# Two more tiles of a gate/up stage by seven block products, and a down dequantization moved into the turns of the tiles

## The chip, the cores and the metric

The kernel runs on one core of a Trainium2 chip. The metric is the device time of one execution in microseconds. Engines: TensorE (PE), VectorE (DVE), ScalarE (ACT), GpSimd (POOL), and SyncE (SP), which only issues DMA.

## What is computed

Two layers, each a residual addition of a conditioned projection and a gated feed-forward. The change touches the first layer's feed-forward. Cut to what matters:

```
GROUP = 128; HIDDEN = 512; INTER = 1376
def _dequant(qw, qz, sc, g_idx):      # 8 nibbles in a word
    wq = unpack_rows(qw); zq = unpack_cols(qz) + 1.0
    return sc[g_idx] * (wq - zq[g_idx])

y = base(x) + 2 * lora(x)                      # 1024 tokens, 512 wide
w_gu = _dequant(qweight_gu, qzeros_gu, scales_gu, g_idx_gu)
gate, up = split(y @ w_gu, INTER)
h = silu(gate) * up
w_d = _dequant(qweight_down, qzeros_down, scales_down, g_idx_down)
x = x + h @ w_d
x = x + layer1(x)     # per-batch 512x512 projection, RMS norm, gated feed-forward of 1792
```

## The kernel before

Everything is computed transposed: features lie on the 128 partitions, the 1024 tokens in two halves of 512 columns. INTER is padded to 11 tiles of 128 (`FT0 = 11`). A float32 product is made of three matmuls: each operand is split into a high part (ScalarE rounds it, `hi`, L746) and a low part (VectorE subtracts, `lo`, L1110), and PE adds high times high, high times low and low times high. So each 128x128 block of weights costs three matmuls of 512 columns for a half of the tokens.

A plain tile of the first gate/up (`gate` and `up`, L1670 to L1674) has 4 blocks for gate and 4 for up, each with both halves: 48 matmuls. A tile in `BLOCK_TILES` (2 to 8 before) is computed by seven block products (`y_product`, L1793 to L1795), a Strassen-Winograd form of 2x2 blocks: seven products of 2 blocks and three matmuls each, 42 matmuls. It needs four sums of weight blocks, on GpSimd (`sums`, L666 to L672), and three additions of products, on VectorE (`y_c_11`, `y_c_12`, `y_c_22`, L1281 to L1291), with copies of products 1, 5 and 6 on ScalarE (`y_snap_1`, `y_snap_5`, `y_snap_2`, L828 to L838).

Each engine has one queue, written out by hand, and goes through it in order. In the turn of block tile i:

- PE runs product 1 of tile i, product 4 of tile i-1, then 5, 2, 6, 3, 7 of tile i. Product 1 waits for the low half of the weights of tile i (`weights_ready`). Product 4 of tile i-1 is added into the bank that `y_c_22` of tile i-1 reads, and waits for it (`s_c22`). Product 3 waits for the copy of product 5 (`s_s5`), product 7 for the copy of product 6 (`s_s2`).
- ScalarE copies product 1, rounds the weights of tile i+1 (`w_hi`, which waits for GpSimd's sums of tile i+1 and for product 4 of tile i-1), copies product 5, rounds h of tile i-1, copies product 6, and does two SiLUs.
- VectorE dequantizes tile i+2 (`dequant_gu`, L1243, one instruction 128x1024), multiplies gate by up for the first half of tile i-1 (`y_mul_0`), makes the low half of the weights of tile i+1 (`w_lo`), the first addition, the low half of h of tile i-1, the second and the third addition, and the second half's product (`y_mul_1`).
- GpSimd makes the sums of a tile as soon as it is dequantized, and gathers the scales by indirect DMA (`gather`, L636).

Tiles 9 and 10 were plain. The down product (`d0_tile`) follows: 6 parts of weights (`e` 0 to 5), whose high and low halves are `w_hi_dn` and `w_lo_dn`. Down weights were dequantized tile by tile (`dequant_dn`, L1253 to L1265) from a gathered row of scales and zeros together (`tab_dn`) and a load of 32-bit words (`load_qd`): five instructions of 512 or 256 columns each, eleven times, all behind the low half of tile 10's weights.

## Time and profile before

| | |
|---|---|
| time, median of 3 runs | 444.44 us (444.4 to 444.64) |
| span of the profiled execution, first to last instruction | 442.5 us |
| PE busy | 438.1 us, 1954 matmuls |
| VectorE busy | 345.7 us, 446 instructions |
| ScalarE, GpSimd busy | 218.7 us, 191.2 us |
| DMA | 79.98 MB, mean 181 GB/s |

The span leaves out what lies around the instructions: the median of the runs is 1.9 us above it (the profiled execution has no other time of its own on record). The first gate/up runs from about 44 to 154 us, the down product to about 214, the second layer to the end.

### The profile page before, as it was taken

The page shows a single profiled execution, that of the slowest core. Times are in us where ns is not written, and L with a number is a line of the kernel's source. Part 1 is how long each engine was busy: PE and PEld are TensorE (multiplying, and loading weights), DVE is VectorE, ACT ScalarE, POOL GpSimd, SP SyncE. Part 2 cuts the span into 40 slices and gives each one's busy share as a digit, 9 for nine tenths or more (in the row PEclk, how much of TensorE's full clock was granted, in tenths as well). Part 3 has the DMA queues.
Part 4 walks back from the last instruction along what each step waited for, and adds up shares of the span by engine and source line. Part 5 has one row for each costly group of instructions (what it writes and reads, how often), then busy time and mean ns, then how long its engine had stood idle before and what let it go on. Part 6 is the DMA issues. An engine that isn't in the chain of part 4 may idle for free.

```text
span 442.5 us, 5522 instructions
## 1 busy us (share of the span) xinstructions
PE 438.1 (99%) x1954; PEld 358.9 (81%) x1954; DVE 345.7 (78%) x446; ACT 218.7 (49%) x285; POOL 191.2 (43%) x162
## 2 busy tenths in 40 slices
...
PEclk9999999999999999999999999999999999999999
...
GB/s 283 221 208 159 23 71 80 86 27 1 1 10 275 199 352 194 143 321 250 97 259 329 219 53 233 320 142 225 214 202 285 62 138 262 346 291 181 217 106 142
DMA packets 30456, 79.98 MB, mean 181 GB/s; under 512 B 2384, under 2 KB 15840, under 8 KB 28768
## 3 DMA queue, kind: packets, MB, share of 16 engines
...
q10 hardware_dynamic: 576, 0.72, 0.5%
...
## 4 chain that ended last, share of the span: by engine, by line
PE 98%; DMA 1%; DVE 0%; issue 0%; DVEq 0%
PE ps L1935 10%; PE ps L1934 10%; PE ps L1933 10%; PE ps L1670 10%; PE ps L1671 10%; PE ps L1674 10%; PE ps L2047 5%; PE ps L2048 5%; PE ps L1794 5%; PE ps L1793 5%; PE ps L2046 5%; PE ps L1795 5%; PE ps L1916 2%; PE ps L1914 2%; PE ps L1915 2%; DMA res<-in_xT 1%
## 5 line engine op out<-in xcount | busy, mean ns | idle before, releaser
L1670 PE MATMUL ps<-h_hi,ring_hi 128*128 128x512 f32 x152 | 59.1, 389 | 0.0
L1671 PE MATMUL ps<-h_lo,ring_hi 128*128 128x512 f32 x152 | 59.1, 389 | 0.0
L1110 DVE TENSOR_TENSOR ring_lo<-raw,ring_hi 128x1792 fp32r<-128x1792 f32 (+3 forms) x24 | 46.5, 1943 | 11.6 <-ACT ring_hi L746 9.4
L1933 PE MATMUL ps<-zt_hi,ring_hi 128*128 128x512 f32 x140 | 54.6, 390 | 0.0
L1935 PE MATMUL ps<-zt_hi,ring_lo 128*128 128x512 f32 x140 | 54.5, 389 | 0.0
L1934 PE MATMUL ps<-zt_lo,ring_hi 128*128 128x512 f32 x140 | 54.5, 389 | 0.0
L1674 PE MATMUL ps<-h_hi,ring_lo 128*128 128x512 f32 x152 | 47.7, 389 | 0.0
L746 ACT ACTIVATE ring_hi<-raw 128x1792 fp32r<-128x1792 f32 (+1 forms) x23 | 36.6, 1593 | 21.1 <-PE ps L1935 10.1
L636 POOL DMA_INDIRECT scale<-in_sc_gu,idx_gu x20 | 25.6, 1280 | 21.7 <-DVE idx_dn L1147 15.9
L1670 PEld LDWEIGHTS ps<-h_hi,ring_hi 128*128 128x128 f32 x152 | 28.5, 188 | 6.0
L1671 PEld LDWEIGHTS ps<-h_lo,ring_hi 128*128 128x128 f32 x152 | 28.5, 188 | 5.9
L1674 PEld LDWEIGHTS ps<-h_hi,ring_lo 128*128 128x128 f32 x152 | 28.5, 188 | 5.9
L1933 PEld LDWEIGHTS ps<-zt_hi,ring_hi 128*128 128x128 f32 x140 | 26.3, 188 | 6.0 <-issue 0.3
L1934 PEld LDWEIGHTS ps<-zt_lo,ring_hi 128*128 128x128 f32 x140 | 26.3, 188 | 5.4
L1935 PEld LDWEIGHTS ps<-zt_hi,ring_lo 128*128 128x128 f32 x140 | 26.3, 188 | 5.4
L672 POOL TENSOR_TENSOR raw<-raw 128x256 f32<-128x256 f32 x19 | 27.9, 1466 | 2.7
L666 POOL TENSOR_TENSOR raw<-raw 128x256 f32<-128x256 f32 x19 | 20.3, 1066 | 19.6 <-DMA raw<-in_gu 11.3
L2048 PE MATMUL ps<-slot,wd 128*128 128x512 f32 (+1 forms) x73 | 27.8, 380 | 0.0
L2046 PE MATMUL ps<-slot,wd 128*128 128x512 f32 (+1 forms) x73 | 27.8, 380 | 0.0
L669 POOL TENSOR_TENSOR raw<-raw 128x256 f32<-128x256 f32 x19 | 26.7, 1404 | 0.0
L636 POOL DMA_INDIRECT dn_work<-in_tab_dn,idx_dn x11 | 12.4, 1123 | 24.5 <-PE ps L1795 21.5
L1518 DVE TENSOR_TENSOR res<-ps,res 128x512 f32<-128x512 f32 (+1 forms) x18 | 10.8, 641 | 15.4 <-PE ps L2048 15.4
...
## 6 DMA issues: line engine op xcount, KB each, us to landing
...
raw<-in_gu SPq DMA_DIRECT2D x12, 512.0 KB, 3.6
...
draw<-in_d SPq DMA_DIRECT2D x7, 512.0 KB, 4.7
...
```

The lines of the kernel that those rows point to most:

```text
L636: pool.indirect_dma_start(dst, None, table, bass.IndirectOffsetOnAxis(ap=index, axis=0)).then_inc(done, 16)
L672: pool.tensor_tensor(s4, a12, s2, ALU.subtract).then_inc(s_sum[4], 1)
L746: act.activation(dst, src, ACT.Copy).then_inc(done, 1)
L1110: dve.tensor_tensor(dst, src, hi_part.bitcast(F32), ALU.subtract).then_inc(done_sem, 1)
L1670: pe.matmul(ps[:, bank + hf, :], w_hi, v_hi[:, t], start=first, stop=False)
L1671: pe.matmul(ps[:, bank + hf, :], w_hi, v_lo[:, t], start=False, stop=False)
L1674: ins = pe.matmul(ps[:, bank + hf, :], w_lo, v_hi[:, t], start=False, stop=last)
L1933: pe.matmul(ps[:, bank, :], ring1_hi[s][:, w], z_hi[:, t], start=first and k == 0, stop=False, skip_group_check=True)
L1934: pe.matmul(ps[:, bank, :], ring1_hi[s][:, w], z_lo[:, t], start=False, stop=False, skip_group_check=True)
L1935: ins = pe.matmul(ps[:, bank, :], ring1_lo[s][:, w], z_hi[:, t], start=False, stop=k == 1, skip_group_check=True)
L2046: pe.matmul(ps[:, bank, c], w_hi, v_hi[:, c], start=k == LAST_K if bank != own else k == 0 and i in (1, 2, 3, 5), stop=False, skip_group_c ...
L2048: return pe.matmul(ps[:, bank, c], w_lo, v_hi[:, c], start=False, stop=k == DH - 1 or (n == 6 and m == 1 and k == LAST_K - 1), skip_group_ ...
```

## The change

Tiles 9 and 10 become block tiles, so that all tiles but 0 and 1 have 42 matmuls. Product 4 of tile 10 is put behind the first 12 matmuls of the down product.

The down weights come as bytes in one load (two nibbles in a byte, 128x1408 words). Their zeros are unpacked with those of gate/up, stored, and gathered by 11 indirect DMAs (`zeros_dn`) between GpSimd's sums of tiles 6 to 9; the scales are gathered by 11 more (`scales_dn`) right into the place where the weights will be. VectorE masks the nibbles once (`nibbles_dn`), adds the zeros once for all tiles (`add_zeros_dn`), and scales in five parts of 2, 2, 2, 2 and 3 tiles (`dequant_dn`). Buffers are laid out anew, and the loads of x and of the first two tiles of the second layer (`res`, `load_pre`) wait for the first part of the down product.

```diff
-BLOCK_TILES = tuple(range(2, FT0 - 2))
+BLOCK_TILES = tuple(range(2, FT0))
 NS = len(BLOCK_TILES)
 S_COL = {B_S1: 8 * P, B_S2: 10 * P, B_S3: 12 * P}
-PLAIN = (0, 1, FT0 - 2, FT0 - 1)
+PLAIN = (0, 1)
 NPAIRS = FT0 // 2
-TD_GROUPS = (2, 2, 4, 3)
+DN_PARTS = ((0, 2), (2, 4), (4, 6), (6, 8), (8, FT0))
...
-            def load_qd(k):
-                sp.dma_start(qd[:, k % 3, :], a["qw_dn"][k, :, :]).then_inc(s_qd[k % 3], 16)
-
-            sp.wait_ge(s_p[7], NS)
-            for k in range(3):
-                load_qd(k)
+            sp.wait_ge(s_zu, 2)
+            sp.dma_start(kept_zd.rearrange("g w -> (g w)").rearrange("(r c) -> r c", c=2 * G_DN), zu[:, ZW // 4:].bitcast(U32)).then_inc(s_zdk, 16)
+            sp.wait_ge(s_zk, 16)
+            sp.wait_ge(s_zdk, 16)
+            sp.dma_start(nib_dn[:, :], a["qw_dn"]).then_inc(s_qd, 16)
...
-            for k in range(3, FT0):
-                sp.wait_ge(s_dn, k - 2)
-                load_qd(k)
-                if k == 8:
-                    sp.wait_ge(s_wf, FT0)
-                    sp.wait_ge(s_hm0, NS)
-                    sp.wait_ge(s_hm1, NS)
-                    sp.dma_start(res[:, :, :], a["xT"]).then_inc(s_xr, 16)
             sp.wait_ge(s_ring, FT0)
             for b in range(2):
                 load_adapter(b)
+            sp.wait_ge(s_hm0, NS)
+            sp.wait_ge(s_hm1, NS)
+            sp.wait_ge(s_ring, FT0 + 1)
+            sp.dma_start(res[:, :, :], a["xT"]).then_inc(s_xr, 16)
 
...
-            sp.wait_ge(s_wlo, FT0)
-            load_pre(0)
-            sp.wait_ge(s_hhi, FT0)
-            sp.wait_ge(s_hlo, FT0)
-            load_pre(1)
+            for g in range(2):
+                load_pre(g)
...
-            def tables_dn(first, last):
+            def zeros_dn(first, last):
 
                 for k in range(first, last):
-                    gather(tab_dn[:, k, :].bitcast(U32), a["tab_dn"], idx_dn[:, k:k + 1], s_td[table_group(k)])
+                    gather(zg_dn[:, D // 4 * k:D // 4 * (k + 1)], kept_zd, idx_dn[:, k:k + 1], s_zgd)
+
+            def scales_dn(g):
+
+                k0, k1 = DN_PARTS[g]
+                for k in range(k0, k1):
+                    gather(dn_tiles(k, k + 1).rearrange("p k n -> p (k n)"), a["sc_dn"], idx_dn[:, k:k + 1], s_td[g])
...
-            for i in BLOCK_TILES[4:]:
-                sums_gu(i)
-            pool.wait_ge(s_p[7], NS)
-            tables_dn(0, 5)
-            pool.wait_ge(s_ring, BLOCK_TILES[-1] + 1)
-            tables_dn(5, FT0)
+            sums_gu(6)
+            pool.wait_ge(s_zdk, 16)
+            zeros_dn(0, 4)
+            sums_gu(7)
+            zeros_dn(4, 8)
+            sums_gu(8)
+            zeros_dn(8, FT0)
+            sums_gu(9)
+            pool.wait_ge(s_wlo, FT0 - 1)
+            for g in range(2):
+                scales_dn(g)
+            sums_gu(10)
+            pool.wait_ge(s_wlo, FT0)
+            for g in range(2, 4):
+                scales_dn(g)
+            pool.wait_ge(s_ring, FT0 - 1)
+            scales_dn(4)
...
             def w_hi_dn(e):
 
-                act.wait_ge(s_wd, (4, 8, FT0)[min(e, 2)])
-                act.wait_ge(*((s_ring, Q["d0"] + e - 1) if e < 5 else (s_htwo, 2)))
-                hi(d0_ring(ring_hi, e), d0_unit(e), s_whi)
+                act.wait_ge(s_wd, (2, 4, 5)[min(e, 2)])
+                if e == 0:
+                    act.wait_ge(s_hm0, NS - 1)
+                    act.wait_ge(s_hm1, NS - 1)
+                else:
+                    act.wait_ge(*((s_ring, Q["d0"] + e - 1) if e < 5 else (s_htwo, 2)))
+                hi(d0_high(e), d0_raw(e), s_whi)
...
             silu(1)
             for i in BLOCK_TILES:
                 y_snap_1(i)
-                w_hi(i + 1)
+                if i + 1 < FT0:
+                    w_hi(i + 1)
+                else:
+                    w_hi_dn(0)
                 y_snap_5(i)
                 h_split(i - 1)
                 y_snap_2(i)
                 y_silu_0(i)
                 y_silu_1(i)
-            w_hi(FT0 - 1)
-            h_split(FT0 - 3)
-            silu(FT0 - 2)
-            w_hi_dn(0)
-            h_split(FT0 - 2)
-            silu(FT0 - 1)
             w_hi_dn(1)
             h_split(FT0 - 1)
 
...
                                          scalar=16.0, in1=scale[j][:, :, 2 * P * s:2 * P * s + 2 * P],
                                          op0=ALU.subtract, op1=ALU.mult).then_inc(s_wf, 1)
 
-            def dequant_dn(k):
-
-                dve.wait_ge(s_td[table_group(k)], 16 * TD_GROUPS[table_group(k)])
-                dve.wait_ge(s_qd[k % 3], 16 * (k // 3 + 1))
-                q = qd[:, k % 3, :]
-                mark(dve.tensor_scalar(q, q, sh32, 15, ALU.logical_shift_right, ALU.bitwise_and))
-                zw = zdp[:, k, 4 * D:4 * D + D // 2]
-                z2 = z_dn.rearrange("p (w e) -> p w e", e=2)
-                need(dve, s_dn, k)
-                mark(dve.tensor_scalar(z2[:, :, 0], zw, 15, None, ALU.bitwise_and))
-                mark(dve.tensor_scalar(z2[:, :, 1], zw, 4, None, ALU.logical_shift_right))
-                dve.wait_ge(s_v, done[0])
-                need(dve, s_wd, k)
-                dve.scalar_tensor_tensor(out=n_dn, in0=q, scalar=1.0, in1=z_dn, op0=ALU.subtract,
-                                         op1=ALU.subtract).then_inc(s_dn, 1)
-                dve.wait_ge(s_dn, k + 1)
-                w = tab_dn[:, k, 0:D]
-                dve.tensor_tensor(w, w, n_dn, ALU.mult).then_inc(s_wd, 1)
+            def nibbles_dn():
+
+                dve.wait_ge(s_qd, 16)
+                dve.tensor_scalar(m_dn[:, :], m_dn[:, :], sh_dn, 0x0F0F, ALU.logical_shift_right, ALU.bitwise_and).then_inc(s_md, 1)
+
+            def add_zeros_dn():
+
+                dve.wait_ge(s_zgd, 16 * FT0)
+                dve.wait_ge(s_md, 1)
+                dve.tensor_tensor(m_dn[:, :], m_dn[:, :], zg_dn.bitcast(U16)[:, :], ALU.add).then_inc(s_md, 1)
+
+            def dequant_dn(g):
+
+                k0, k1 = DN_PARTS[g]
+                w = dn_tiles(k0, k1)
+                dve.wait_ge(s_md, 2)
+                dve.wait_ge(s_td[g], 16 * (k1 - k0))
+                dve.scalar_tensor_tensor(out=w, in0=nib_dn[:, D // 4 * k0:D // 4 * k1].bitcast(U8).rearrange("p (k n) -> p k n", n=D),
+                                         scalar=16.0, in1=w, op0=ALU.subtract, op1=ALU.mult).then_inc(s_wd, 1)
 
             def gate_times_up(i):
...
             y_sum_lo(4)
             h_split(0)
             for i in BLOCK_TILES:
-                dequant_gu(i + 2)
+                if i + 2 < FT0:
+                    dequant_gu(i + 2)
                 if i > 2:
                     y_mul_0(i - 1)
                 else:
                     gate_times_up(i - 1)
-                w_lo(i + 1)
+                if i + 1 < FT0:
+                    w_lo(i + 1)
+                else:
+                    w_lo_dn(0)
+                if i == 7:
+                    nibbles_dn()
+                if i == 9:
+                    add_zeros_dn()
                 y_c_11(i)
+                if i == 9:
+                    dequant_dn(0)
                 h_split(i - 1)
                 y_c_12(i)
+                if i == 9:
+                    dequant_dn(1)
+                if i == FT0 - 1:
+                    dequant_dn(2)
                 y_c_22(i)
                 y_mul_1(i)
-            y_mul_0(FT0 - 3)
-            w_lo(FT0 - 1)
-            h_split(FT0 - 3)
-            for k in range(4):
-                dequant_dn(k)
-            gate_times_up(FT0 - 2)
-            w_lo_dn(0)
-            h_split(FT0 - 2)
-            for k in range(4, 8):
-                dequant_dn(k)
+            dequant_dn(3)
+            y_mul_0(FT0 - 1)
+            dequant_dn(4)
             w_lo_dn(1)
-            gate_times_up(FT0 - 1)
             h_split(FT0 - 1)
 
...
                 y_p_6(i)
                 y_p_3(i)
                 y_p_7(i)
-            weights_ready(FT0 - 2)
-            banks_free(NS - 1)
-            gate(FT0 - 2, range(1))
-            y_p_4(FT0 - 3)
-            gate(FT0 - 2, range(1, KD))
-            up(FT0 - 2)
-            weights_ready(FT0 - 1)
...
-                w_hi, w_lo = d0_ring(ring_hi, e), d0_ring(ring_lo, e)
...
+                        y_p_4(FT0 - 1)
                     if pr == 1 and k % 2:
```

How the order moves, with the engine's rows as the program has them (tiles are named by what they write and read, `snap_1` is the odd tiles' buffer; lines of the changed kernel are 6 to 20 higher).

VectorE before, from the low half of tile 9's weights: the turn of tile 8 and what followed it.

```order
L1110 TENSOR_TENSOR ring_lo<-raw_1,ring_hi 128x1024 [waits s_whi]
L1281 TENSOR_TENSOR snap_0<-ps,snap_0 128x512 [waits s_s1,s_p2]
L1110 TENSOR_TENSOR h_lo<-h_raw,h_hi 128x1024 [waits s_hhi]
L1286 TENSOR_TENSOR snap_0<-ps,snap_0 128x512 [waits s_s2,s_p3]
L1291 TENSOR_TENSOR snap_0<-ps,snap_0 128x512 [waits s_s5,s_p7]
L1301 TENSOR_TENSOR h_raw<-snap_0 128x512 [waits s_c22,s_silu1]
L1296 TENSOR_TENSOR h_raw<-snap_0,ps 128x512 [waits s_ring,s_silu0]
L1110 TENSOR_TENSOR ring_lo<-raw_0,ring_hi 128x1024 [waits s_whi]
L1110 TENSOR_TENSOR h_lo<-h_raw,h_hi 128x1024 [waits s_hhi]
L1253 TENSOR_SCALAR dn_work<-dn_work,cst 128x512 [waits s_qd0,s_td0]
L1257 TENSOR_SCALAR zn_dn<-dn_work 128x256
```

VectorE in the change, from the low half of tile 10's weights: the turn of tile 9.

```order
L1127 TENSOR_TENSOR ring_lo<-raw_0,ring_hi 128x1792 [waits s_whi]
L1274 TENSOR_TENSOR nib_dn<-nib_dn,zg_dn 128x2816 [waits s_md,s_zgd]
L1299 TENSOR_TENSOR snap_1<-ps,snap_1 128x512 [waits s_s1,s_p2]
L1282 SCALAR_TENSOR_TENSOR w_dn<-nib_dn,w_dn 128x1024 [waits s_td0,s_md]
L1127 TENSOR_TENSOR h_lo<-h_raw,h_hi 128x1024 [waits s_hhi]
L1304 TENSOR_TENSOR snap_1<-ps,snap_1 128x512 [waits s_s2,s_p3]
L1282 SCALAR_TENSOR_TENSOR w_dn<-nib_dn,w_dn 128x1024 [waits s_td1,s_md]
L1309 TENSOR_TENSOR snap_1<-ps,snap_1 128x512 [waits s_s5,s_p7]
L1319 TENSOR_TENSOR h_raw<-snap_1 128x512 [waits s_c22,s_silu1]
L1314 TENSOR_TENSOR h_raw<-snap_1,ps 128x512 [waits s_ring,s_silu0]
```

The first addition now follows the addition of all zeros, and a scaling of two tiles stands before h's low half and another before the third addition (L1309), for which PE's product 4 waits. The turn of tile 7 has the nibbles (one row of 128x2816) in the same place as the zeros here, and the turn of tile 10 a third scaling before its third addition.

GpSimd before, from the first sum of tile 7 on.

```order
L666 TENSOR_TENSOR raw_1<-raw_1 128x256 [waits s_wf]
L667 TENSOR_TENSOR raw_1<-raw_1 128x256
L669 TENSOR_TENSOR raw_1<-raw_1 128x256 [waits s_sum1]
L672 TENSOR_TENSOR raw_1<-raw_1 128x2x128 [waits s_sum2,s_sum3]
L666 TENSOR_TENSOR raw_0<-raw_0 128x256 [waits s_wf]
L667 TENSOR_TENSOR raw_0<-raw_0 128x256
L669 TENSOR_TENSOR raw_0<-raw_0 128x256 [waits s_sum1]
L672 TENSOR_TENSOR raw_0<-raw_0 128x2x128 [waits s_sum2,s_sum3]
L636 DMA dn_work<-in_tab_dn,idx_dn 128x576 [waits s_p7]
L636 DMA dn_work<-in_tab_dn,idx_dn 128x576 x4
L636 DMA dn_work<-in_tab_dn,idx_dn 128x576 [waits s_ring]
L636 DMA dn_work<-in_tab_dn,idx_dn 128x576 x5
```

GpSimd in the change, from the last sum of tile 8 on.

```order
L678 TENSOR_TENSOR raw_0<-raw_0 128x2x128 [waits s_sum2,s_sum3]
L636 DMA zg_dn<-zeros_dn,idx_dn 128x128 x3
L672 TENSOR_TENSOR raw_1<-raw_1 128x256 [waits s_wf]
L673 TENSOR_TENSOR raw_1<-raw_1 128x256
L675 TENSOR_TENSOR raw_1<-raw_1 128x256 [waits s_sum1]
L678 TENSOR_TENSOR raw_1<-raw_1 128x2x128 [waits s_sum2,s_sum3]
L636 DMA w_dn<-in_sc_dn,idx_dn 128x512 [waits s_wlo]
L636 DMA w_dn<-in_sc_dn,idx_dn 128x512 x3
L672 TENSOR_TENSOR raw_0<-raw_0 128x256 [waits s_wf]
L673 TENSOR_TENSOR raw_0<-raw_0 128x256
L675 TENSOR_TENSOR raw_0<-raw_0 128x256 [waits s_sum1]
L678 TENSOR_TENSOR raw_0<-raw_0 128x2x128 [waits s_sum2,s_sum3]
```

Eleven gathers of zeros now stand between the sums of tiles 6 and 9 (four, four and three), and four of scales, which wait for the low half of tile 9's weights, before the sums of tile 10.

## Rows read from the trace of the kernel before

**Rows 1.** The page, part 1 (engines) and part 2 (40 slices).
```profile
PE 438.1 (99%) x1954; PEld 358.9 (81%) x1954; DVE 345.7 (78%) x446; ACT 218.7 (49%) x285; POOL 191.2 (43%) x162
...
PEclk9999999999999999999999999999999999999999
```

**Rows 2.** Waits of PE: line, waited for, us in total, times, longest.
```profile
PE ps L1681 <- DVE zn_dn L1112: 1.2, 1, 1.2
PE ps L1683 <- DMA res<-in_xT: 0.4, 1, 0.4
PE ps L1712 <- DVE aw_hi L1126: 0.2, 1, 0.2
```

**Rows 3.** Timeline of PE: first matmuls of tiles 6, 7, down product.
```profile
102.30 0.39 PE L1793 MATMUL ps<-h_hi,ring_hi 128*128 128x512 f32 x1
...
111.82 0.39 PE L1793 MATMUL ps<-h_hi,ring_hi 128*128 128x512 f32 x1
...
153.98 0.39 PE L1670 MATMUL ps<-h_hi,ring_hi 128*128 128x512 f32 x1
```

**Rows 4.** Timeline of VectorE (DVE) in the turn of tile 7.
```profile
116.56 2.03 DVE L1110 TENSOR_TENSOR ring_lo<-raw,ring_hi 128x1792 fp32r<-128x1792 f32 x1 [1.06 <-ACT ring_hi L746]
118.50 0.68 DVE L1281 TENSOR_TENSOR snap<-ps,snap 128x512 f32<-128x512 f32 x1
119.10 1.22 DVE L1110 TENSOR_TENSOR h_lo<-h_raw,h_hi 128x1024 fp32r<-128x1024 f32 x1
120.23 0.69 DVE L1286 TENSOR_TENSOR snap<-ps,snap 128x512 f32<-128x512 f32 x1
121.54 0.69 DVE L1291 TENSOR_TENSOR snap<-ps,snap 128x512 f32<-128x512 f32 x1 [0.62 <-PE ps L1795]
```

**Rows 5.** Timeline of ScalarE (ACT) in the turn of tile 7.
```profile
114.82 1.71 ACT L746 ACTIVATE ring_hi<-raw 128x1792 fp32r<-128x1792 f32 x1 [0.84 <-PE ps L1795]
116.43 0.58 ACT L838 ACTIVATE snap<-ps 128x512 f32<-128x512 f32 x1
```

**Rows 6.** Timeline of VectorE: nibbles, zeros (1024, 1536 wide), scaling.
```profile
27.08 1.87 DVE L1211 TENSOR_SCALAR nib<-nib,cst 128x2560 uint16<-128x2560 uint16 x2
...
33.87 0.69 DVE L1218 TENSOR_TENSOR nib<-nib,zg 128x1024 uint16<-128x1024 uint16 x1
...
41.69 0.95 DVE L1218 TENSOR_TENSOR nib<-nib,zg 128x1536 uint16<-128x1536 uint16 x1
...
113.42 1.22 DVE L1243 SCALAR_TENSOR_TENSOR raw<-nib,scale 128x1024 f32<-128x1024 uint8 x1
```

**Rows 7.** Groups of GpSimd (POOL) by form: the eleven gathers of before.
```profile
L636 POOL DMA_INDIRECT dn_work<-in_tab_dn,idx_dn x11 | 12.4, 1123 | 24.5 <-PE ps L1795 21.5 <-issue 3.0
```

**Rows 8.** Timeline of GpSimd: first and last sums, tiles 6 and 8.
```profile
90.86 1.80 POOL L666 TENSOR_TENSOR raw<-raw 128x256 f32<-128x256 f32 x1
...
94.19 1.00 POOL L672 TENSOR_TENSOR raw<-raw 128x256 f32<-128x256 f32 x1
...
105.20 0.74 POOL L666 TENSOR_TENSOR raw<-raw 128x256 f32<-128x256 f32 x1 [3.19 <-DVE raw L1243]
...
107.47 2.34 POOL L672 TENSOR_TENSOR raw<-raw 128x256 f32<-128x256 f32 x1
```

**Rows 9.** Timelines of VectorE and GpSimd: a subtraction beside a gather.
```profile
61.54 2.01 DVE L1110 TENSOR_TENSOR ring_lo<-raw,ring_hi 128x1792 fp32r<-128x1792 f32 x1
...
61.76 2.62 POOL L636 DMA_INDIRECT scale<-in_sc_gu,idx_gu  x1 [0.30 <-issue]
```

**Rows 10.** Timeline of VectorE: last low half; issues by size, landing: two loads.
```profile
202.15 0.95 DVE L1110 TENSOR_TENSOR ring_lo<-dn_work,ring_hi 128x768 fp32r<-128x768 f32 x1
...
res<-in_xT SPq DMA_DIRECT2D x1, 2048.0 KB, 9.0
...
pre_raw<-in_gu SPq DMA_DIRECT2D x2, 512.0 KB, 9.1
```

**Rows 11.** Timeline of PE: the warm-up matmuls at the start.
```profile
1.21 3.19 PE L1681 MATMUL ps<-zn_dn 128*128 128x512 bf16 x8 [1.21 <-DVE zn_dn L1112]
```

More of the change, by code:

```diff
@@ L282, in build @@
         s_idx, s_zg, s_aok = (sem(n) for n in ("s_idx", "s_zg", "s_aok"))
-        s_td = [sem(f"s_td{c}") for c in range(len(TD_GROUPS))]
+        s_td = [sem(f"s_td{g}") for g in range(len(DN_PARTS))]
+        s_zdk, s_zgd, s_md = sem("s_zdk"), sem("s_zgd"), sem("s_md")
         s_sc = [sem(f"s_sc{c}") for c in range(3)]
@@ L291, in build @@
         s_qw = sem("s_qw")
-        s_qd = [sem(f"s_qd{s}") for s in range(3)]
+        s_qd = sem("s_qd")
         s_nib, s_zu, s_n, s_wf = (sem(n) for n in ("s_nib", "s_zu", "s_n", "s_wf"))
-        s_dn, s_wd = sem("s_dn"), sem("s_wd")
+        s_wd = sem("s_wd")
         s_whi = sem("s_whi")
@@ L424, in z_block, with d0_cols, d0_raw, d0_low @@
             return zt_hi[:, Z_OF[i], :], zt_lo[:, Z_OF[i], :]
-        def d0_unit(e):
-            pr, c = divmod(e, len(D0_CHUNK))
-            k0 = sum(D0_CHUNK[:c])
-            return tab_dn[:, k0:k0 + D0_CHUNK[c], BLK * pr:BLK * pr + BLK]
-        def table_group(k):
-            return sum(k >= sum(TD_GROUPS[:c]) for c in range(1, len(TD_GROUPS)))
-        def d0_ring(ring, e):
-            n = BLK * D0_CHUNK[e % len(D0_CHUNK)]
-            return ring[:, (FT0 + e) % 2, 0:n].rearrange("p (k n) -> p k n", n=BLK)
+        def d0_cols(e):
+            pr = e // len(D0_CHUNK)
+            return slice(BLK * pr, BLK * pr + BLK)
+        def d0_raw(e):
+            return w_dn[e % len(D0_CHUNK)][:, :, d0_cols(e)]
+        def d0_low(e):
+            return w_dn_lo[e % len(D0_CHUNK)][:, :, d0_cols(e)]
+        def d0_high(e):
+            n = BLK * D0_CHUNK[e % len(D0_CHUNK)]
+            return d0_hi[1 + (e - 1) % 2 if e else 0][:, 0:n].rearrange("p (k n) -> p k n", n=BLK)
+        def dn_tiles(k0, k1):
+            c = sum(k0 >= sum(D0_CHUNK[:c]) for c in (1, 2))
+            at = sum(D0_CHUNK[:c])
+            return w_dn[c][:, k0 - at:k1 - at, :]
         def h1_tile(low, high, i):
```

69 lines of the change are left out of this document (32 added, 37 removed).

## The prediction

> **What bounds the kernel now.** I read the page first: PE is busy for 438.1 of 442.5 us, at a granted clock of full speed in every slice (the 2.4 GHz level) [rows 1]. Then the waits of PE: three in the whole execution, 1.8 us together, all before the first real product [rows 2]. So PE runs without a pause from about 5 us to the end, and every matmul taken away shortens the kernel by its pitch, as long as the other engines still come in time. The pitch comes from PE's timeline: tile 6 starts at 102.30, tile 7 at 111.82, 42 matmuls later [rows 3], so 9.52 / 42 = 0.2267 us each. The same rhythm gives tile 8 at 121.34, tile 9 at 130.86, tile 10 (in its new form) at 140.38; in the old form the down product starts at 153.98 [rows 3], 102 matmuls after 130.86.
>
> **What is removed from PE.** Tiles 9 and 10 go from 48 matmuls to 42 each; product 4 of tile 8 was there already and product 4 of tile 10 is inside its 42. That is 12 x 0.2267 = **-2.72 us**, on the path, certain.
>
> **What is removed from VectorE.** The down weights were dequantized by five instructions a tile, 55 in all, behind the low half of tile 10. PE waited for none of them [rows 2], so taking them away gives nothing back. What counts is where their 7 replacements stand: the order puts them into the turns of tiles 7, 9 and 10, in front of additions for which PE waits. The eleven loads and eleven gathers of before were hidden for the same reason.
>
> **How little slack a block tile has.** PE's queue in tile i runs products 1, 4 of tile i-1, 5, 2, 6, 3, 7 of 1.36 us each (6 x 0.2267). Product 4 of tile i-1 waits for VectorE's third addition of that tile. For tile 7 it starts at 121.34 + 1.36 = 122.70 and the addition ends at 121.54 + 0.69 = 122.23 [rows 4]: 0.47 us early. Without VectorE's own waits its chain from the low half of the next weights (116.56, ends about 118.5) through first addition 0.60, low half of h 1.13, second addition 0.60 and third 0.69 takes 3.02 us, so could end at 121.5: **1.2 us is all that can be inserted there**. ScalarE rounds the next weights in 1.71 us when product 4 is done (114.82) and, behind that on its queue, copies product 5 (116.43, ends 117.0) [rows 5]; product 3 of that tile (111.82 + 6.80 = 118.62) waits for this copy, so **the block sums of the next tile may be 1.6 us late**.
>
> **Prices of what is added.** VectorE: the nibbles of the down weights are 128x2816 in 16 bits; the first gate/up has 5632 columns (11 tiles of 512), masked by two instructions in 1.87 us [rows 6], so half of that is 0.95. The zeros, an addition of 128x2816 in 16 bits: 1024 take 0.69, 1536 take 0.95, so 0.52 ns an element and 1.6 us. A scaling of two tiles (128x1024, bytes times f32) is the form that took 1.22, 1.14 start to start [rows 6]; the last, of three tiles, about 1.7. GpSimd: a gather takes 1.12 on the mean plus 0.30 of issue, 1.42 us [rows 7]; the sums of a tile took 4.33 (90.86 to 95.19) and 4.61 (105.20 to 109.81), I take 4.5; undisturbed they would be 4 x 0.74 = 3.0 [rows 8]. A gather was held to 2.62 us while VectorE subtracted two SBUF tensors (61.54 to 63.55) [rows 9]; that is the upper end. The Trainium skill (SBUF — State Buffer, "Who interferes with whom") calls this an exclusive lock of the port pair that VectorE and GpSimd share. By that rule a gather that starts in the free time costs 0.95, the gathers come off at 5.0 us a group, and wait 1 below falls to almost nothing; the trace agrees that gathers differ by what VectorE runs.
>
> **Wait 1, tile 7's product 4.** The gathers stand ahead of sums on GpSimd. Sums of tile 6 end at 95.19. Four gathers 5.7: 100.9. Sums of 7: 105.4. Four gathers: 111.1. Sums of 8: 115.6, 0.8 later than ScalarE wants them (114.82). ScalarE's copy still fits. VectorE's low half then ends at 119.3; nibbles to 120.25; the chain of 3.02 to 123.3, due at 122.70: **0.6 us** (0 to 2).
>
> **Wait 2, tile 9's product 3.** Three gathers and sums of 9: 124.4, in time. The first four gathers of the scales wait for the low half of tile 9: product 4 of tile 7 ends at 124.7, ScalarE's 1792-wide rounding at 126.6, the low half at 128.6. They end at 134.3, and only then come the sums of tile 10, with VectorE idle beside them: 137.3. ScalarE rounds to 138.9, copies product 5 to 139.45. PE wants product 3 at 131.46 + 6.80 = 138.3: **1.2 us**, and 0.1 more before product 7, whose bank waits for ScalarE's next copy. With slow sums it is 2.7; with undisturbed gathers about 0.
>
> **Wait 3, tile 9's product 4.** The low half of tile 10 ends at 140.95. Then stand zeros 1.6, first addition 0.6, scaling 1.14, low half of h 1.13, second addition 0.6, scaling 1.14, third addition 0.69: 147.9, and 0.1 to PE. PE has done products 3, 7 and tile 10's first by 143.65: **4.3 us**. Were GpSimd always in time, the low half would end at 137.5 and PE want product 4 at 141.74: still 2.8. This is the wait I am surest of, since 3.9 us are put into a place with 1.2.
>
> **Behind that.** Tile 10's product 4 stands behind twelve matmuls of the down product, so the scaling put before its third addition has 1.36 us more and costs nothing. Down weights for the later parts have over 5 us each. SyncE now loads x and the two first L1 tiles 12.2 us into the down product, not in its first 7; the row that would suffer is the last low half of the down weights, 202.15 + 0.95, due 228 matmuls after 153.98 at 205.67 [rows 10], so 2.6 us early, and 1.36 more through the product inside; the loads (9 us to landing) make it late by less than 2. The early 0.7 MB load stands beside the gathers of the first zeros, added at 33.87 [rows 6], ten us ahead of tile 0's first product: nothing.
>
> **Sum.** -2.72 + 0.6 + 1.3 + 4.3 = +3.5 us. The traced execution spans 442.5, hence 446.0; the median of the runs, 444.44, is 1.9 above the span, so **448.0 us**. A measurement of this kernel tells 0.2%, 0.9 us, from no change.
>
> **Rivals.** *A, faster:* VectorE's insertions are hidden after all. It decides at wait 3: if the zeros and two scalings together took under 1.2 us and GpSimd is in time, no wait is left and the time is 441.7; up to 3.0 us of insertions (1.8 us of wait) it stays faster by over 0.2%. Against it: 3.9 us from like forms [rows 6], and PE's fixed order of products. *B, GpSimd in time:* the gathers cost 1.25 and sums 3.0 to 4.3, waits 1 and 2 vanish, 2.8 stay: -2.7 + 2.8, 444.5. For it: the undisturbed gathers and sums of 0.74 [rows 8]; against it, that GpSimd would then be busy 8 to 9.3 of 9.52 us in three turns running. *C, GpSimd becomes the bound:* one gather in each group of four is held as in [rows 9], 1.5 us more. Wait 1 grows by 3.0, since two groups add up before it, wait 2 by 1.5: 452.4. For it: VectorE subtracts SBUF tensors for 3 to 4 us of each tile's turn. Against it: the mean of the eleven gathers of before was 1.12 [rows 7]. *D, the clock falls after wait 3.* PE has not stood for 4 us here since the start, where after 1.2 us of idle eight matmuls of 512 columns took 3.19 us, so 0.40 from start to start, (3.19 - 0.39) / 7, against 0.227, the nearest rows for the lower level of 1.2 GHz [rows 2, 11]. Eight such cost 1.4 us, sixteen 2.8: 449.4 to 450.8. The Trainium skill (TensorE: Matmul & The Clock Gate, "Why this matters for your kernels") warns of idle gaps above about 3 us between bursts of matmuls, after which the clock is halved. By it this rival would be the likely one; no row of this trace has such a gap, so I leave it at 0.13. That tiles 9 and 10 are not changed as told is excluded by the diff of `BLOCK_TILES` and by the order of PE, where each now has 42 matmuls.
>
> **How the numbers follow.** Forecast 0.50, B 0.15, C 0.12, D 0.13, A 0.08, worse than C 0.02. The range goes from just under B to C, 444.2 to 452.6, and leaves out A and what is beyond C, 0.1 together, with a little of C. B is mostly within 0.2%: faster 0.08, same 0.10, slower 0.82.
>
> **What would show it.** PE with 12 fewer matmuls; PE waits for a VectorE addition once for about 4 us near 144 us, which is wait 3; for a ScalarE copy for about 1 us near 138; for an addition for under 1 us near 123. GpSimd's sums of tile 10 start after 134. From the down product on PE has no wait. It is wrong if PE's wait near 144 is under 2 us, if waits appear after 160 us, or if the granted clock falls.

## The result, and the profile after

| | before | after |
|---|---|---|
| median of 4 runs, us | 444.42 (444.18 to 444.64) | 454.78 (454.02 to 457.13) |
| ratio, 95% interval | | 1.0239 [1.0222, 1.0257] |
| profiled execution: span, us | 442.5 | 453.5 |
| matmuls of PE in the trace | 1954 | 1942 |
| mean granted clock | 1.00 | 0.989 |

Slower by 10.4 us where 3.6 were forecast (448.0), and outside the range, which ended at 452.6. The long waits of PE after (line, waited for, us in total, times, longest), where before only the start had any [rows 2]:

```profile
PE ps L1815 <- DVE snap L1309: 6.5, 2, 3.9
PE ps L1815 <- ACT snap L859: 1.7, 2, 1.1
PE ps L1703 <- DVE zeros L1129: 1.2, 1, 1.2
```

L1309 is the third addition of a tile (`y_c_22`), L859 ScalarE's copy of product 5. Tile 6 still starts at 102.28, where it started at 102.30 [rows 3], so all that PE loses lies behind it. PE's timeline, the first matmul of each product that waits and its surroundings:

```profile
118.37 0.39 PE L1817 MATMUL ps<-yt_hi,ring_lo 128*128 128x512 f32 x1
119.89 0.50 PE L1815 MATMUL ps<-h_hi,ring_hi 128*128 128x512 f32 x1 [1.13 <-ACT snap L859]
...
124.03 0.39 PE L1817 MATMUL ps<-h_hi,ring_lo 128*128 128x512 f32 x1
126.98 0.47 PE L1815 MATMUL ps<-yt_hi,ring_hi 128*128 128x512 f32 x1 [2.56 <-DVE snap L1309]
127.29 0.53 PE L1816 MATMUL ps<-yt_lo,ring_hi 128*128 128x512 f32 x1
...
128.04 0.63 PE L1815 MATMUL ps<-yt_hi,ring_hi 128*128 128x512 f32 x1
...
130.60 0.50 PE L1815 MATMUL ps<-yt_hi,ring_hi 128*128 128x512 f32 x1
...
144.34 0.50 PE L1815 MATMUL ps<-h_hi,ring_hi 128*128 128x512 f32 x1 [0.55 <-ACT snap L859]
...
148.46 0.39 PE L1817 MATMUL ps<-h_hi,ring_lo 128*128 128x512 f32 x1
152.75 0.76 PE L1815 MATMUL ps<-yt_hi,ring_hi 128*128 128x512 f32 x1 [3.90 <-DVE snap L1309]
...
158.00 0.45 PE L1815 MATMUL ps<-h_hi,ring_hi 128*128 128x512 f32 x1
...
163.55 0.39 PE L1692 MATMUL ps<-h_hi,d_hi 128*128 128x512 f32 x1
```

Four waits stand here. Taken from the start of one matmul to the start of the next, less the pitch of 0.227 us, they are 1.29, 2.72, 0.71 and 4.06, together 8.8 us. And behind the second and the fourth the distance between matmuls is 0.43 instead of 0.227 us. The stretches (columns: us, busy of PE, weight loads, VectorE, ScalarE, GpSimd, granted clock, DMA share, GB/s):

```profile
119.00:127.20 8.20, 4.75 (x19) 3.47 (x20) 7.71 (x7) 3.84 (x7) 6.75 (x6) 1.00 0.20 24
127.30:130.70 3.40, 3.40 (x10) 2.65 (x9) 2.16 (x3) 1.15 (x2) 0.00 (x0) 0.51 0.00 0
130.70:144.00 13.30, 13.09 (x58) 10.52 (x56) 7.32 (x8) 6.44 (x9) 7.27 (x8) 1.00 0.31 80
144.00:153.00 9.00, 4.77 (x19) 3.51 (x20) 8.89 (x9) 3.47 (x6) 5.49 (x4) 0.90 0.31 78
153.00:158.20 5.20, 5.20 (x13) 4.04 (x14) 1.67 (x3) 1.06 (x1) 1.74 (x2) 0.51 0.32 81
```

The granted clock is 0.51 there, the level of 1.2 GHz. From 127.29 to 130.60 eight steps take 3.31 instead of 1.81 us, from 152.75 to 158.00 twelve take 5.25 instead of 2.72: 4.0 us for the clock. **The balance closes:** at the old pitch the down product would start at 102.28 + 210 x 0.2267 = 149.9 (the 210 matmuls of tiles 6 to 10; product 4 of tile 10 comes later). It starts at 163.55, 13.7 late: 8.8 waits, 4.0 clock, 0.9 in small steps of 0.04 to 0.11 around each wait and in rounding. And 442.5 - 2.7 + 13.7 = 453.5, the span. From the down product on nothing was gained or lost.

Why so late? GpSimd, the turns of tiles 6 and 7, where before stood [rows 8] and no gathers:

```profile
95.33 1.76 POOL L636 DMA_INDIRECT zg_dn<-zeros_dn,idx_dn  x1 [0.15 <-issue]
97.40 0.95 POOL L636 DMA_INDIRECT zg_dn<-zeros_dn,idx_dn  x1 [0.30 <-issue]
98.65 1.70 POOL L636 DMA_INDIRECT zg_dn<-zeros_dn,idx_dn  x1 [0.30 <-issue]
100.65 1.43 POOL L636 DMA_INDIRECT zg_dn<-zeros_dn,idx_dn  x1 [0.30 <-issue]
102.10 0.75 POOL L672 TENSOR_TENSOR raw<-raw 128x256 f32<-128x256 f32 x1
...
105.53 1.76 POOL L636 DMA_INDIRECT zg_dn<-zeros_dn,idx_dn  x1 [0.15 <-issue]
107.60 2.45 POOL L636 DMA_INDIRECT zg_dn<-zeros_dn,idx_dn  x1 [0.30 <-issue]
...
113.04 1.27 POOL L672 TENSOR_TENSOR raw<-raw 128x256 f32<-128x256 f32 x1
...
116.83 0.74 POOL L678 TENSOR_TENSOR raw<-raw 128x256 f32<-128x256 f32 x1
...
122.42 0.75 POOL L672 TENSOR_TENSOR raw<-raw 128x256 f32<-128x256 f32 x1
...
124.69 1.53 POOL L678 TENSOR_TENSOR raw<-raw 128x256 f32<-128x256 f32 x1
```

A group of four gathers takes 6.8 us (95.33 to 102.10) and 7.5 us (105.53 to 113.04); I had 5.7. What the first group took too long, the sums of tile 7 made up for (3.4 us from 102.10 to the next gather, where I had 4.5), so the second group, 1.8 us over, is what was left of it in tile 8. The sums of tile 8 end at 117.57 instead of 109.81 [rows 8]; the forecast had 115.6. What follows from that on ScalarE and VectorE:

```profile
117.65 1.70 ACT L763 ACTIVATE ring_hi<-raw 128x1792 fp32r<-128x1792 f32 x1 [3.70 <-POOL raw L678]
119.26 0.58 ACT L859 ACTIVATE snap<-ps 128x512 f32<-128x512 f32 x1
```

```profile
107.20 2.02 DVE L1127 TENSOR_TENSOR ring_lo<-raw,ring_hi 128x1792 fp32r<-128x1792 f32 x1
...
119.39 2.02 DVE L1127 TENSOR_TENSOR ring_lo<-raw,ring_hi 128x1792 fp32r<-128x1792 f32 x1 [3.39 <-ACT ring_hi L763]
121.33 0.95 DVE L1268 TENSOR_SCALAR nib_dn<-nib_dn,cst 128x2816 uint16<-128x2816 uint16 x1
122.19 0.68 DVE L1299 TENSOR_TENSOR snap<-ps,snap 128x512 f32<-128x512 f32 x1
122.79 2.84 DVE L1127 TENSOR_TENSOR h_lo<-h_raw,h_hi 128x1024 fp32r<-128x1024 f32 x1
125.56 0.68 DVE L1304 TENSOR_TENSOR snap<-ps,snap 128x512 f32<-128x512 f32 x1
126.16 0.68 DVE L1309 TENSOR_TENSOR snap<-ps,snap 128x512 f32<-128x512 f32 x1
...
145.78 1.62 DVE L1274 TENSOR_TENSOR nib_dn<-nib_dn,zg_dn 128x2816 uint16<-128x2816 uint16 x1
147.31 0.68 DVE L1299 TENSOR_TENSOR snap<-ps,snap 128x512 f32<-128x512 f32 x1
147.92 1.22 DVE L1282 SCALAR_TENSOR_TENSOR w_dn<-nib_dn,w_dn 128x1024 f32<-128x1024 uint8 x1
...
151.91 0.69 DVE L1309 TENSOR_TENSOR snap<-ps,snap 128x512 f32<-128x512 f32 x1
```

ScalarE rounds 2.8 us later than before [rows 5], and the copy behind it is then late for product 3. The low half of h took 1.22 us a turn earlier. Here it takes 2.84 (122.79 to 125.63), beside GpSimd's sums of tile 9 (122.42 to 126.22). The other direction shows at 107.60, where a gather took 2.45 beside the subtraction of 107.20, as in [rows 9]. So each of the two engines is slow beside certain work of the other. The nibbles, the zeros and the scalings cost what was forecast: 0.95, 1.62, 1.22.

### The profile page after: what moved, and what is told of

Same layout as the page of the kernel before. It is cut to its first block, busy times and chain, and to the rows that moved or that the text cites. A ratio compares the mean times of both kernels' runs of the same rounds, so it can differ in the third digit from the quotient of the medians.

```text
span 453.5 us, 5486 instructions
## 1 busy us (share of the span) xinstructions
PE 441.3 (97%) x1942; PEld 359.0 (79%) x1942; DVE 336.5 (74%) x406; ACT 223.1 (49%) x293; POOL 207.7 (46%) x181
## 4 chain that ended last, share of the span: by engine, by line
PE 73%; POOL 11%; DVE 8%; issue 3%; ACT 2%; DMA 1%; DVEq 0%; ACTq 0%; POOLq 0%
PE ps L1947 10%; PE ps L1948 10%; PE ps L1949 10%; PE ps L1692 6%; PE ps L1696 6%; PE ps L1693 6%; PE ps L2061 5%; PE ps L2060 5%; PE ps L2062 5%; POOL zg_dn L636 3%; POOL raw L672 2%; DVE h_lo L1127 2%; PE ps L1930 2%; PE ps L1928 2%; PE ps L1929 2%
## 5 line engine op out<-in xcount | busy, mean ns | idle before, releaser
L1127 DVE TENSOR_TENSOR ring_lo<-raw,ring_hi 128x1792 fp32r<-128x1792 f32 (+3 forms) x24 | 47.6, 1989 | 17.1 <-ACT ring_hi L763 14.8
L763 ACT ACTIVATE ring_hi<-raw 128x1792 fp32r<-128x1792 f32 (+1 forms) x23 | 37.9, 1649 | 25.9 <-PE ps L1949 10.1
L1815 PE MATMUL ps<-yt_hi,ring_hi 128*128 128x512 f32 x72 | 29.9, 416 | 6.5 <-DVE snap L1309 6.5
L1692 PE MATMUL ps<-h_hi,d_hi 128*128 128x512 f32 x88 | 34.2, 389 | 0.0
L1693 PE MATMUL ps<-h_lo,d_hi 128*128 128x512 f32 x88 | 34.2, 389 | 0.0
L672 POOL TENSOR_TENSOR raw<-raw 128x256 f32<-128x256 f32 x21 | 24.1, 1146 | 15.3 <-DMA raw<-in_gu 11.5
L1817 PE MATMUL ps<-yt_hi,ring_lo 128*128 128x512 f32 x72 | 29.7, 413 | 0.0
L1816 PE MATMUL ps<-yt_lo,ring_hi 128*128 128x512 f32 x72 | 29.6, 411 | 0.0
L1696 PE MATMUL ps<-h_hi,w_dn_lo 128*128 128x512 f32 x88 | 28.1, 389 | 0.0
L678 POOL TENSOR_TENSOR raw<-raw 128x256 f32<-128x256 f32 x21 | 26.3, 1253 | 3.0
L675 POOL TENSOR_TENSOR raw<-raw 128x256 f32<-128x256 f32 x21 | 26.4, 1257 | 0.0
L673 POOL TENSOR_TENSOR raw<-raw 128x256 f32<-128x256 f32 x21 | 26.1, 1242 | 0.0
L730 POOL TENSOR_TENSOR ad_lo<-ad_raw,ad_hi 128x1024 fp32r<-128x1024 f32 x1 | 2.4, 2406 | 48.6 <-ACT ad_hi L763 48.6
```

The lines of the kernel that those rows point to most:

```text
L672: pool.tensor_tensor(s1, a21, a22, ALU.add).then_inc(s_sum[1], 1)
L763: act.activation(dst, src, ACT.Copy).then_inc(done, 1)
L1127: dve.tensor_tensor(dst, src, hi_part.bitcast(F32), ALU.subtract).then_inc(done_sem, 1)
L1692: pe.matmul(ps[:, bank + hf, :], w_hi, v_hi[:, t], start=first, stop=False)
L1693: pe.matmul(ps[:, bank + hf, :], w_hi, v_lo[:, t], start=False, stop=False)
L1696: ins = pe.matmul(ps[:, bank + hf, :], w_lo, v_hi[:, t], start=False, stop=last)
```

## The experiments

Three theories stood after this. **Places:** VectorE's steps stand in front of additions PE waits for. **GpSimd:** it is the bound in three turns, since the gathers stand ahead of the sums. **Clock:** part of the loss is not waiting but slow matmuls behind a wait. Each run is compared with the kernel before on the same chip. That took 444.62 us for the runs with the copy first, one insertion back and the late load, 444.48 for those with the wait near 143 filled, the gathers back and two insertions back, and 444.47 for the other four.

### VectorE's steps of turn 9 behind the third addition

```
...
 y_c_22(i)
+if i == 9: add_zeros_dn()
 y_mul_1(i)
+if i == 9: dequant_dn(0); dequant_dn(1)
...
```

(and their old places dropped.)

> VectorE's three insertions of the turn of tile 9 (zeros addition, first and second scaling) move behind the third addition for which PE waits; GpSimd's order and the nibbles stay. Theory (gaps plus clock): the wait of 3.9 us near 153 goes and the low clock behind it (3.4 us) with it, the waits near 120 to 127 (3.7 us), the low clock behind them (1.7 us) and the 0.5 us near 144 stay. 454.8 - 3.9 - 3.4 = 447.5 us (446.5 to 448.5). Rival 'the wait comes from GpSimd's late sums' (the low half of tile 10's weights is 2.9 us later than I reckoned): then 2 us or more of the wait stay and with them the low clock, 451 to 453 us. Rival 'the clock falls whatever PE does here': only the wait goes, 450.9 us.

Measured: 450.81 us (449.78 to 451.92), ratio 1.0119 [1.0059, 1.0178]. The wait of 3.9 us near 153 and the slow matmuls behind it are gone, 6.6 us. But only 3.4 come off the span. The time is that of the rival by which only the wait would go (450.9), but the trace does not bear it out: behind 132.64 no row of matmuls up to the down product has the distance of 0.43 us. What was missing stands in its waits of PE:

```profile
PE ps L1815 <- ACT snap L859: 3.2, 4, 1.1
PE ps L1815 <- DVE snap L1309: 2.6, 1, 2.6
```

ScalarE's copy is late four times instead of twice: in tile 6 already, in tile 7, in tile 9, and in tile 10, where it stands behind the rounding of the first down weights, which waits for the scaling that I had moved back. The first of these comes from nothing that was edited: in this execution two gathers of scales at 76.00 and 79.45 took 1.89 and 2.17 us where they took 0.95 after, and GpSimd reached its four gathers of zeros 1 us later, with the group of 7.5 us now one tile earlier. So how the two engines fall beside each other can differ from execution to execution of one order, and with it where PE waits. "Places" is right for the wait near 153; the forecast missed by the copies.

### GpSimd: sums first

```
...
-zeros_dn(0, 4); sums_gu(7); zeros_dn(4, 8); sums_gu(8); zeros_dn(8, FT0); sums_gu(9)
+zeros_dn(0, 1); sums_gu(7); zeros_dn(1, 3); sums_gu(8); zeros_dn(3, 6); sums_gu(9)
+zeros_dn(6, FT0)
+sums_gu(10)
 pool.wait_ge(s_wlo, FT0 - 1)
 for g in range(2): scales_dn(g)
-sums_gu(10)
...
```

> Only GpSimd's order changes: one, two, three and five gathers of zeros behind the sums of tiles 6, 7, 8 and 9 instead of four, four and three behind 6, 7 and 8, and the sums of tile 10 ahead of the gathers of scales. VectorE's places stay. Theory: the waits for ScalarE's copy (1.1 near 120, 0.5 near 144) go, the one near 127 shrinks from 2.6 to 0 to 0.6 (the nibbles alone put 0.95 into a place with 1.2 us), and its low clock (1.7) goes; the wait near 153 shrinks to about 2.8. If the clock falls behind a wait of 2.8 us too: 454.8 - 1.1 - 0.5 - 2.3 - 1.7 - 1.1 = 448.1 us; if it does not fall there, 3.4 less, 444.7 us. Rival 'the gathers are slow wherever they stand and hold VectorE': waits of 2 us and more stay near 127 and the time is over 450 us.

Measured: 447.44 us (445.47 to 449.8, 12 runs), 1.0064 [1.0047, 1.008]. As the first theory had it: no wait for ScalarE is left, the one near 123 is 0.3, and one of 3.1 stays at tile 9's product 4, with nine steps from 145.72 to 149.44 behind it, 3.72 us instead of 2.04 (first the waits of PE, then its timeline).

```profile
PE ps L1816 <- DVE snap L1310: 3.4, 2, 3.1
```

```profile
145.72 0.62 PE L1816 MATMUL ps<-yt_hi,ring_hi 128*128 128x512 f32 x1 [3.08 <-DVE snap L1310]
...
149.44 0.39 PE L1816 MATMUL ps<-yt_hi,ring_hi 128*128 128x512 f32 x1
```

The same program hints at what the clock costs: eight of the twelve executions have a mean granted clock of 0.996 (spans 445.3 to 448.0, median 445.8), four of 1.00 (443.7, 444.0, 444.2 and 446.8, median 444.1). That is the same order, 1.7 us apart, and 1.7 is also what the nine slow steps cost. Only one of the twelve was profiled, so that the wait was as long in the others isn't shown.

### Matmuls in place of the waits

The kernel after, with matmuls that nobody reads ahead of product 4 of tiles 7 and 9:

```
...
 y_p_1(i)
+for _ in range({8: 10, FT0 - 1: 15}.get(i, 0)):
+    pe.matmul(ps[:, 3, :], warm[:, 0:P], warm, start=True, stop=True)
 y_p_4(i - 1)
...
```

> Adds matmuls whose result nobody reads (zeros times zeros, bf16, 512 columns, into a bank that is started afresh before its next use): 10 ahead of product 4 of tile 7 and 15 ahead of product 4 of tile 9, so that PE works through 2.3 of the 2.6 us and 3.4 of the 3.9 us in which it stood there. Nothing else changes, and the additions it waits for are as late as before. Theory 'part of the loss is the clock': it stays at full speed, 1.7 + 3.4 = 5.1 us come back and 0 to 0.5 us go to matmuls that outlast the wait: 449.7 to 450.5 us. Rival 'the clock falls for another reason than PE's standing still (a limit on power, the state of the chip)': no gain, 454.5 to 455.5 us.

Measured: 452.92 us (451.33 to 456.56), 1.0166 [1.0112, 1.022]. The clock stays at 1.00 in all five executions (0.999 or above), where all four of the kernel after had 0.989 or 0.992. So the clock fell because PE stood. But only 1.9 us of the 4.0 come back in the median (5.1 were expected), 3.5 in the best run, and the two kernels' times overlap. The profiled execution, the slowest of the five, shows where they go:

```profile
PE ps L1815 <- ACT snap L859: 2.6, 3, 1.1
PE ps L1692 <- DVE gates L1242: 2.4, 1, 2.4
```

```profile
36.04 0.50 PE L1692 MATMUL ps<-act_hi,w0b_hi 128*128 128x512 f32 x1 [2.43 <-DVE gates L1242]
...
36.61 0.39 PE L1692 MATMUL ps<-act_hi,w0b_hi 128*128 128x512 f32 x1
36.84 0.40 PE L1693 MATMUL ps<-act_lo,w0b_hi 128*128 128x512 f32 x1
```

The copy is late for product 3 of tiles 6, 7 and 9 (1.1, 0.6, 0.9 us; after, 1.13 at tile 7 and 0.55 at tile 9): in tile 6 as in the run with VectorE's steps of turn 9 moved, with the same two slow gathers of scales (1.89 and 2.22 us), and in tile 9 more than after, which fits PE at full speed coming there earlier while GpSimd doesn't. **What the clock gives back is partly waited for at the next late engine.** The 2.4 us belong to the start of this execution alone (36.04): VectorE stood for 5.16 us before 34.76 and the trace names nothing on the chip for it. That is taken up below. Behind these 2.43 us of standing the clock did not fall: it was granted at 1.00 from 36.04 to 40, and the matmuls keep their 0.23 us (36.61 to 36.84), where in the kernel after it fell behind 2.56.

### The wait near 143 alone filled

Sums first, and 14 such matmuls ahead of product 4 of tile 9.

> The run with the sums first (447.44 us, one wait of 3.1 us near 142.6, then eight matmuls at 1.2 GHz), and 14 matmuls whose result nobody reads (bf16 zeros, 512 columns) ahead of product 4 of tile 9, 3.2 us of work in place of the wait. VectorE and GpSimd are as late as before. Theory: full clock throughout, 447.44 less the eight slow matmuls' 1.7 us is 445.7, or 0.2 to 0.4 above that for the matmuls' own end. Rival 'the clock falls for another reason': 447.4 or above.

Measured: 446.25 us (445.9 to 446.86), 1.0038 [1.0025, 1.0051], clock 1.00 in all six. 1.2 us faster than without the matmuls (1.7 expected); in the profiled execution the wait near 123 was 1.25 instead of 0.30 us. With GpSimd out of the way most of the clock's share comes back.

### VectorE's steps at the heads of the turns

Sums first on GpSimd, and on VectorE:

```
...
 dequant_gu(i + 2)
+if i == 9: add_zeros_dn()
+if i == FT0 - 1: dequant_dn(0); dequant_dn(1)
 y_mul_0(i - 1)
+if i == 8: nibbles_dn()
 w_lo(i + 1)
...
```

(and the old places dropped: the nibbles one turn later, zeros and scalings where VectorE waits for ScalarE's rounding.)

> GpSimd's order as in the run with the sums first, and on VectorE every inserted step at the head of a turn, where it waits for ScalarE anyway: nibbles ahead of the low half in turn 8, zeros addition at the head of turn 9, the two first scalings at the head of turn 10. Theory: no wait of PE is left from 5 us on, full clock throughout, so 454.8 - 8.8 - 5.1 = 440.9, or 444.4 - 2.7 = 441.7 by the sum from before: 441 to 442.5 us, faster than before by 0.6%. Rival 'the head of a turn is not free either' (the turn of VectorE is 9.5 us long and nearly full): one wait of 1 to 2 us is left, 443 to 444.5 us.

Measured: 443.98 us (442.68 to 446.78, 12 runs), 0.9988 [0.9959, 1.0016]: level with before, and the time of the rival. One wait of 0.8 us was left in the profile, product 3 of tile 10, behind the rounding of the down weights on ScalarE. The zeros took 2.16 us there instead of 1.62, beside GpSimd's last sum of a tile and a gather.

### The copy ahead of the rounding

```
...
 y_snap_1(i)
 if i + 1 < FT0: w_hi(i + 1)
-else: w_hi_dn(0)
 y_snap_5(i)
+if i == FT0 - 1: w_hi_dn(0)
...
```

> As the run with both new places, and on ScalarE the copy of product 5 of tile 10 stands ahead of the rounding of the first down weights instead of behind it. There that copy was at 148.17, behind a rounding at 147.21 that had waited for the second scaling (145.30), and product 3 of tile 10 waited 0.81 us. Theory: this wait goes, 443.98 - 0.9 = 443.1 us. Rival 'the rounding and its low half are then late for the down product': a wait of 0.5 us or more behind 150 us and no gain, 443.5 to 444.5.

Measured: **442.67 us** (441.82 to 443.4, 12 runs), **0.995 [0.9933, 0.9967]**, faster than before by 1.95 us (444.62), 0.4%. PE's waits and the stretches:

```profile
PE ps L1703 <- DVE zeros L1130: 1.2, 1, 1.2
```

```profile
102.00:122.00 20.00, 20.00 (x90) 16.50 (x89) 17.15 (x17) 11.20 (x14) 18.18 (x16) 1.00 0.17 18
122.00:150.00 28.00, 27.91 (x123) 22.65 (x122) 24.11 (x26) 15.62 (x21) 23.90 (x18) 1.00 0.34 85
```

No wait behind the start, full clock. Of the 2.72 us of twelve matmuls 1.95 arrive. In the profiled execution tile 6 started 0.4 us later than before (102.68), and 0.5 went into small steps between it and the down product. GpSimd is busy for 18.2 of 20 us between 102 and 122: it fits, with nothing to spare.

### The gathers back in their old order

The same, with GpSimd's order of the change.

> As the run with the copy first, but GpSimd's order is that of the change (four, four and three gathers of zeros behind the sums of tiles 6, 7 and 8, four gathers of scales ahead of the sums of tile 10); VectorE's steps stay at the heads of the turns. It prices GpSimd's order alone. Theory: the copy's wait near 120 (1.1 us) stays, product 4 of tile 7 waits 2.6 less 0.95 for the nibbles, 1.6 us, and product 3 of tile 9 about 0.5 to 1: 3.2 to 3.7 us in all and no slow clock, 446 to 446.5 us. Rival 'GpSimd is late only because VectorE's insertions hold it': waits under 1 us, 443 to 443.7 us. Rival 'the clock falls': 447.7 us or more.

Measured: 448.42 us (446.38 to 449.24), 1.0073 [1.0054, 1.0091]. 5.8 us more than with the sums first, for the order of the gathers alone:

```profile
PE ps L1814 <- ACT snap L859: 3.6, 2, 2.5
PE ps L1814 <- DVE snap L1309: 0.4, 1, 0.4
```

The sum of the waits was nearly right (4.0 against 3.2 to 3.7), their places were not: product 3 of tile 9 waits 2.46 us, since PE comes there earlier than in the kernel after (0.55). ScalarE's rounding for tile 9 waited there until 127.37 for GpSimd's sums of that tile, which the forecast had in time at 124.4; in the kernel after it waited for PE instead. And behind these 2.46 the clock falls too (0.996 in five of six executions): the rival of 447.7 us and more is the one that came.

### One insertion back, and two

From the run with the copy first. One: the zeros back ahead of the first addition of tile 9 (with the load of the nibbles late, below). Two: zeros and the first scaling back.

> As the run with the late load, but the zeros addition stands back where the change put it, ahead of the first addition of tile 9; the two scalings stay at the head of turn 10. It prices one insertion alone: 1.6 us (2.2 if GpSimd holds it) into a place with 1.2 us of slack is a wait of 0.4 to 1.0 us near 142, and none of the clock behind it: slower than the late-load run by 0.4 to 1.0 us. Rival 'any wait in this stage halves the clock': 1.7 us more, 2.1 to 2.7 us slower.

> As the run with the copy first, but the zeros addition and the first scaling stand where the change put them (ahead of the first addition and of the low half of h in turn 9), the second scaling stays at the head of turn 10. 1.6 + 1.14 us into a place with 1.2 us of slack (less 0.1 to 0.4 for what the addition measured with it alone): a wait of 1.4 to 2.0 us near 143, half of the one of 3.1 with both scalings. Theory 'the clock falls only behind a longer wait': 442.7 + 1.6 = 444.3 us, no row of 0.43 us pitch behind it. Rival 'it falls here too': 1.7 us more, 446.0. A rise of less than 1 us would say that PE's later waits (about 0.5 near 149) take up part of it.

Measured: one, 442.7 us (442.17 to 445.16), 0.9956 [0.9938, 0.9973], a wait of 0.5 us at 143.37 and no gain or loss against 442.76 without it; the gap of 0.47 us at 149.35 of that run is gone instead. Two, 443.94 us (443.41 to 444.31), 0.9984 [0.9976, 0.9993], one wait:

```profile
144.36 0.47 PE L1816 MATMUL ps<-yt_hi,ring_hi 128*128 128x512 f32 x1 [1.47 <-DVE snap L1310]
```

1.47 us for 2.76 inserted (1.62 and 1.14): the slack of 1.2 us is confirmed to 0.1. The clock is 1.00 in all twelve executions. So the series at this place: 1.6 us inserted cost nothing, 2.8 cost 1.3 us of time (1.4 when each is set against before on its own chip), and 3.9 (the run with the sums first, which has the nibbles and ScalarE's copy in their old places too) cost a wait of 3.1 and mostly 1.7 for the clock, 4.8 in all.

### The load of the nibbles later

The 0.7 MB load behind PE's tile 2 instead of at 24 to 26 us.

> As the run with the copy first, and the 0.7 MB load of the nibbles of the down weights is issued when PE has done with tile 2 (about 73 us) instead of at 24 to 26 us. Theory 'the early load disturbs the start': runs of the variants spread over 3 to 5 us (440.9 to 445.0 of span at full clock) where those of before spread over 1, and one profile shows VectorE standing 5.16 us at 29.6 to 34.8, for nothing on the chip that the trace names, with PE waiting 2.4 us at 36. With the load late the spread shrinks to about 1 us and the median is 441.6 to 442.2 us. Rival 'the spread comes from the joined zeros table or the gathers': the same spread and the median of the run with the copy first, 443 us.

Measured: 442.76 us (442.16 to 447.0, 12 runs), 0.9968 [0.9943, 0.9994]. The rival holds: same median, and two executions of twelve at 446.6 and 447.0 though the load was late; the kernel before, on the same chip, had five of 29 at 445.4 to 448.0 as well. The early load is not the cause of the spread, and the standing of VectorE near 30 us stays open.

## Why the prediction was wrong, point by point

By one of its own signs it failed outright: the granted clock fell. Step by step:

- **Removed from PE**, 12 x 0.2267: right. The balance closes with it to 0.1 us, and the best order brings 1.95 of it home.
- **Wait 3** (tile 9's product 4), "the wait I am surest of", 4.3 us: right, 3.9. Its prices and its slack too; with GpSimd in time I had 2.8, measured 3.1.
- **Wait 1** (0.6, with "ScalarE's copy still fits"): wrong, and the first step that failed. It measured 1.3 at the copy and 2.7 at product 4. The rule was right: block sums "may be 1.6 us late". They were 2.75 late (117.57 against 114.82), and product 3 waited 1.13, the difference. What was mis-sized is the term "four gathers 5.7": 6.8 and 7.5. I had taken the mean of eleven gathers of before [rows 7], and put into a turn of VectorE full of subtractions, some of them were as slow as the one of [rows 9]: 0.94 to 2.45 us, median 1.43, and 0.3 of issue each. Rival C had a chance of 0.12; its mechanism, held gathers, is the one that came, and with its 3.0 us wait 1 would be 3.6, against 4.0 measured. That these numbers are so close is partly luck: GpSimd was 2.0 us later than forecast (117.57 against 115.6), not 3.0. The other 1.6 is what no rival had, the other direction: the low half of h took 2.84 us instead of 1.22 while GpSimd worked.
- **Wait 2** (1.2): 0.55, smaller, for two reasons. The four gathers of scales took 4.8 us (133.67 to 138.47) and not 5.7, beside no 1792-wide subtraction of VectorE. And PE itself was late, which hid that the sums of tile 9 were late too. The run with the gathers back shows 2.46 where PE is on time, so for a PE without delay the forecast was too small, and "sums of 9: 124.4, in time" was wrong.
- **The clock** (rival D, 0.13, priced at 1.4 to 2.8 for one fall): it fell twice, 4.0 us. Two steps failed. I looked for a fall only behind wait 3, since wait 1 was thought to be 0.6; and I left D at 0.13 because no row of before had such a gap, though the Trainium skill (TensorE: Matmul & The Clock Gate, "Why this matters for your kernels") warns of such gaps. A page that speaks to what the trace can't show should have had the larger chance. The bound of about 3 us of idle that the Trainium skill gives there is not what these runs show: the clock fell behind 2.56 and 2.46 us too, though not behind 2.43 in another run.
- **The sum.** Forecast +3.5 = -2.7 + 6.2. Measured +11.0 in the span: waits 8.8 (6.2 forecast), clock 4.0 (none), small steps 0.9 (none); 13.7 - 2.7. Of the 7.5 us between the two, wait 1 is 3.4, the clock 4.0 and the small steps 0.9, and waits 2 and 3 give 0.8 back.
- **Behind the down product**: right, no wait.
- **Rival A**, insertions hidden, was wrong for this order and right for another: with every step at the head of a turn 442.67 us, against 441.7 by the sum (with ScalarE's copy moved too).

GpSimd's order alone costs 5.8 us and VectorE's places (with ScalarE's copy) 4.8, each from the best version; together 12.1 (454.78 - 442.67), 1.6 more than their sum. These runs were on different chips; set against before on the same chip, the three figures are 5.9, 4.9 and 12.3, 1.5 more than the sum. Each of the two runs has one fall of the clock in its profile, the kernel after two. They cost 1.7 us each there (nine slow steps), and 1.5 and 2.5 in the kernel after (eight and twelve), so the clock makes 0.6 of the 1.6. The rest is open.

Not tried: which instruction of VectorE slows which gather, and the cause of the executions that are 3 to 4 us longer at full clock.
